# Graph convolution with residual and layer norm: zero fills read from memory, a paced order of the fills, and copies moved into the products

## The reference

```python
def _edge_conv(x, src, dst, edge_attr, W, b, denom):
    msg = jnp.concatenate([x[src], edge_attr], axis=1) @ W + b
    s = jax.ops.segment_sum(msg, dst, num_segments=x.shape[0])
    return s / denom[:, None]
...
h = _edge_conv(x, src, dst, edge_attr, W0, b0, denom)
outputs = [h]
for W, b in ((W1, b1), (W2, b2), (W3, b3)):
    cat = jnp.concatenate(outputs, axis=1)
    z = _edge_conv(cat, src, dst, edge_attr, W, b, denom)
    outputs.append(z)
return outputs[-1]
...
x = _layernorm(x + _L0_gnn_ref(...), axis=-1)
```

## Time and profile before

| | |
|---|---|
| time, median of 3 executions | 1039.77 us (1036.18 to 1040.24) |
| the profiled execution | 1047.12 us, its span 1045.2 us |
| busy share of the span | POOL 69%, DVE 67%, ACT 48%, PE 46% |
| DMA, mean over the span | 215 GB/s |
| TensorE clock granted, mean | 0.659 of full speed |

### The profile page before, as it was taken

The page is one execution under the profiler, slowest core; times in us unless marked ns, Lnnn a source line. Parts: engine busy times, 40 slices in busy tenths (PEclk is TensorE's granted clock), DMA queues, the critical chain, the costliest instruction groups (busy, mean ns, idle before and its releaser), DMA issues.

```text
span 1045.2 us, 13945 instructions
## 1 busy us (share of the span) xinstructions
PE 482.6 (46%) x3072; PEld 360.4 (34%) x3072; DVE 696.5 (67%) x2390; ACT 499.3 (48%) x1322; POOL 725.2 (69%) x660
## 2 busy tenths in 40 slices
PE   3343654877874797998663600260026563000000
PEld 2343553655653465664332500250025452000000
DVE  6995888777755696658456585757579973699000
ACT  5552674766551565666452226732675640275200
POOL 6684776777770577777576468766878774777775
PEclk9655665655655889998886655565557876555555
DMA  6799569599996356775458459985999981654111
GB/s 183 231 283 265 149 162 270 156 327 312 324 347 230 137 186 206 243 242 172 162 203 277 159 131 292 310 277 118 299 300 366 320 292 47 197 159 142 51 50 34
DMA packets 224619, 224.98 MB, mean 215 GB/s; under 512 B 19218, under 2 KB 206475, under 8 KB 224495
## 3 DMA queue, kind: packets, MB, share of 16 engines
q1 hardware_dynamic: 193551, 153.22, 47.2%
q0 software_dynamic: 26624, 44.81, 15.8%
q10 hardware_dynamic: 4320, 25.56, 6.1%
HBM read 117.11 MB, written 132.74 MB: 239 GB/s over the span
## 4 chain that ended last, share of the span: by engine, by line
DVE 20%; POOL 19%; DMA 19%; PE 17%; issue 12%; SPq 5%; ACT 5%; DVEq 2%; POOLq 0%; ACTq 0%
POOL G L670 5%; POOL out_rows L709 5%; SPq L487 4%; POOL part_rows L683 4%; DMA area<-src_low_rows 3%; DMA G<-part_rows,s0r 3%; DMA x_and_z_of_nodes<-area,sum_rows 3%; PE hp L1909 3%; DMA G<-x_in,srci 3%; PE segp L1909 2%; DVE area L1035 2%; PE hp L2049 2%; POOL G L641 2%; DVE AC L1583 2%; ACT area L809 2%
## 5 line engine op out<-in xcount | busy, mean ns | idle before, releaser
L641 POOL DMA_INDIRECT G<-x_in,srci x196 | 221.2, 1129 | 84.9 <-issue 55.6
L653 POOL DMA_INDIRECT x_and_z_of_nodes<-area,sum_rows x144 | 145.6, 1011 | 89.8 <-ACT area L809 61.7
L837 ACT ACTIVATE area<-area,AC 128x128 f32<-128x128 f32 x299 | 117.5, 479 | 43.0 <-DVE AC L1605 43.0
L778 ACT ACTIVATE UT<-segp,UT 128x1 f32 x168 | 44.0, 262 | 119.6 <-PE segp L1808 92.7
L670 POOL DMA_INDIRECT G<-part_rows,s0r x70 | 81.0, 1157 | 23.6 <-issue 18.3
L1808 PE MATMUL segp<-SX,G 128*128 128x128 f32 x336 | 83.1, 430 | 15.0 <-DMA G<-x_in,srci 11.7
L809 ACT ACTIVATE area<-hp,zero,inv 128x512 f32<-128x512 f32 x72 | 53.7, 777 | 66.6 <-DMA x_and_z_of_nodes<-area,sum_rows 32.0
L702 POOL DMA_INDIRECT EC<-x_and_z_of_nodes,idx x60 | 63.8, 1063 | 28.9 <-issue 16.5
L2043 PE MATMUL segp<-ZERO 128*128 128x390 f16 (+1 forms) x34 | 14.2, 418 | 147.4 <-DVE EC L1625 147.4
L1808 PEld LDWEIGHTS segp<-SX,G 128*128 128x128 f32 x336 | 73.3, 322 | 18.0 <-DMA G<-x_in,srci 14.2
L709 POOL DMA_INDIRECT out_rows<-UT,idx x60 | 59.1, 985 | 18.3 <-issue 17.7
(11 more groups left out here) (464 smaller groups left out, 1504.3 us busy)
## 6 DMA issues: line engine op xcount, KB each, us to landing
part_rows<-area SPq DMA_DIRECT2D x36, 768.0 KB
area<-x_and_z_of_nodes SPq DMA_DIRECT2D x30, 832.0 KB, 7.5
x_and_z_of_nodes<-ZERO SPq DMA_DIRECT2D x24, 1024.0 KB
x_and_z_of_nodes<-x_in SPq DMA_DIRECT2D x24, 1024.0 KB
area<-x_in SPq DMA_DIRECT2D x23, 832.0 KB, 7.8
out_rows<-area ACTq DMA_DIRECT2D x23, 832.0 KB, 5.1
part_rows<-ZERO SPq DMA_DIRECT2D x14, 768.0 KB
area<-src_low_rows SPq DMA_DIRECT2D x28, 224.0 KB
```

What stands on the lines that cost most here:

```text
L641: g.indirect_dma_start(G[:, slot, 0:D], None, x, bass.IndirectOffsetOnAxis(ap=srci[:, c:c + 1].bitcast(u32), axis=0), bounds_check=last_no ...
L653: g.indirect_dma_start(XZ2, bass.IndirectOffsetOnAxis(ap=sum_rows[:, c:c + 1], axis=0), HS3[:, b, j, 3 * D:4 * D], None, bounds_check=last ...
L837: last = a.activation(XLS[b][:, k], XLS[b][:, k], ACT.Identity, bias=shift[:, b, r:r + 1], scale=rs[:, b, r:r + 1])
```

## The change

It does four things. A table `ZD` (zero_rows, 128 rows of 384 zeros) is made in memory from `ZERO`, once, before the first piece, and SP waits for it; all later zeros are read from `ZD`. The order of the pieces of `clear_sums` is another: 4 at the start and 4 behind the first rows of low bits, as before; then, in place of 10 in one run ahead of the remaining 26 rows, one behind every second row (13 in all), and 4 at the end. Of `copy_x`, 12 pieces stay in the front and 13 go behind the stores of the products' steps; they count on a semaphore of their own, `copied`, for which POOL waits ahead of its last gathers. The zeros for `TB` go out behind the stores too: the part for step k in step k x 18 / 25, so that the 14 that are sent here fall into the last five steps.

```diff
-Z_AT = (4, 8, 18)
+Z_FIRST, Z_LOOKS = 8, 13
+X_FRONT = 12
...
+    ZD = nc.dram_tensor("zero_rows", [P, 3 * D], f32).ap()
...
+            e.dma_start(ZD, ZERO[:, 0:3 * D]).then_inc(s["zeros_in"], 16)
...
-                    e.dma_start(run_rows(XZ3[:, 1, :], lo, hi), ZERO[0:rows, 0:D].unsqueeze(1).to_broadcast([rows, XRUN, D])).then_inc(s["cleared"], 16)
+                    e.dma_start(run_rows(XZ3[:, 1, :], lo, hi), ZD[0:rows, 0:D].unsqueeze(1).to_broadcast([rows, XRUN, D])).then_inc(s["cleared"], 16)
...
-                    e.dma_start(run_rows(XZ3[:, 0, :], lo, hi), run_rows(x, lo, hi)).then_inc(s["cleared"], 16)
-
-            clear_sums(range(0, Z_AT[0]))
+                    e.dma_start(run_rows(XZ3[:, 0, :], lo, hi), run_rows(x, lo, hi)).then_inc(s["copied"], 16)
+
+            share = lambda n, parts, j: range(n * j // parts, n * (j + 1) // parts)
+
+            e.wait_ge(s["zeros_in"], 16)
+            clear_sums(range(0, Z_FIRST // 2))
...
-            clear_sums(range(Z_AT[0], Z_AT[1]))
+            clear_sums(range(Z_FIRST // 2, Z_FIRST))
             e.wait_ge(s["we_ready"], 1)
             for q in (0, 1):
                 load_features(q)
-            clear_sums(range(Z_AT[1], Z_AT[2]))
             for c in range(2, UNITS):
                 load_lows(c)
-            clear_sums(range(Z_AT[2], XPIECES))
+                clear_sums(Z_FIRST + p for p in share(Z_LOOKS, UNITS - 2, c - 2))
+            clear_sums(range(Z_FIRST + Z_LOOKS, XPIECES))
             for q in range(2, NQ):
                 load_features(q)
-                copy_x(range((q - 2) * XPIECES // (NQ - 2), (q - 1) * XPIECES // (NQ - 2)))
+                copy_x(share(X_FRONT, NQ - 2, q - 2))
             e.wait_ge(s["prep_done"], 1)
             n_fill = e.value_load(counts[0:1, 0:1], min_val=1, max_val=CIT)
-            for i in range(CIT):
+
+            def fill_unused(i):
                 with e.If(n_fill <= i):
                     for g in (i * 2, i * 2 + 1):
-                        e.dma_start(trows[g], ZERO[:, 0:3 * D].unsqueeze(1).to_broadcast([P, CG, 3 * D])).then_inc(s["zfill"], 16)
+                        e.dma_start(trows[g], ZD.unsqueeze(1).to_broadcast([P, CG, 3 * D])).then_inc(s["zfill"], 16)
+
...
+                copy_x(X_FRONT + p for p in share(XPIECES - X_FRONT, SLOTS, i))
+                for k in share(CIT, SLOTS, i):
+                    fill_unused(k)
                 e.sem_inc(s["tick_sp"], 1)
...
-            e.wait_ge(s["cleared"], 2 * 16 * XPIECES)
+            e.wait_ge(s["cleared"], 16 * XPIECES)
...
+            e.wait_ge(s["copied"], 16 * XPIECES)
             l_units(gather_final)
```

More of the change, by code:

```diff
@@ L355, in gnn_kernel @@
             "flags_in flags_mm order_known ld_bc ld_sort sort_dve rank_ready sorted "
-            "prep_done rows_known ut_clear zrow zfill we_ready "
+            "prep_done rows_known ut_clear zrow zeros_in zfill we_ready "
             "far row_built summed "
@@ L363, in gnn_kernel @@
             "oh_built tab_mm tab_ready os_built hot_words look_mm looked words_in a_built a_mm a_added list_ready "
-            "p_mm p_act weights_mm weights_in sc_ready cleared "
+            "p_mm p_act weights_mm weights_in sc_ready cleared copied "
             "places_known lows_turned lows_copied lows_stored chunks_ready mk_built mk_mm marked tb_ready lk_built lk_mm found2 c2_hot c2_built c2_mm c2_added "
```

## The result

The changed kernel takes 1080.95 us, the median of 4 runs (1079.54 to 1081.09); the kernel before took 1040.01 beside it (1036.18 to 1043.70). The ratio is 1.0388, with a 95% interval of 1.0345 to 1.0430: slower by 41 us, where 19 were forecast. The profiled execution took 1080.92, with a span of 1078.9.

A forecast was written before the change was run, and what follows sets the result against it. Bounds taken: row 2's wait behind ten pieces, then DVE's look-ups; in the products POOL's scatters and ACT's waits for them. Front +2, products +4 and +9, tail +4: +19 on 1047.1, 1066, or 1059 on the runs' scale; range 1033 to 1086.

The forecast's parts named there:

- The wait goes: Front: row 2 goes out at 88.8 and lands at 92.3 instead of 99.5, -7 us.
- Zeros from memory: All pieces and fills: zeros read from memory move as fast as from SBUF, priced by the copies' 323 GB/s; no difference.
- the last rival: Much slower: all pieces read the same 192 KB, a bottleneck at half the rate; +85 us, 1125; chance 0.10.
- The pacing: Look-ups: each later row pair stands behind a piece, 1.78 MB at 318 GB/s, 5.6 us a pair; +12 us.
- The front's end: End of the front: fills gone, the last gather's landing falls from 6.4 toward 3.5 us; -3, bounds 0 and -3.
- The products: Nine copies in steps 1 to 12 crowd scatters, +4 (0 to +9); stores wait behind fills in steps 13 to 17, +9.
- Behind the last store: Gap before the rounds: POOL waits for the last copy and 4 fills, first gather 15.2 us after the store; +4.
- the look-ups' share: Sign in the look-ups: the stretch should show a DMA share over 1.
- POOL's first gap after them: Sign behind the look-ups: POOL's first gap should come later by about 5 us.
- the others: Signs: DVE's chunk 2 wait 2 to 3.5 us; products +13, mostly after step 13, ACT waiting; POOL's first rounds gather awaits fills.
- The rivals of a gain: Faster: zeros from memory let the DMA engines reach 430 GB/s, the front gains 10; 1031 us; chance 0.18.
- the rival of no change: 374 GB/s throughout and scatters don't wait for copies: pacing 3, front gains 7, drain 5, tail 3; 1041 us; chance 0.16.

The follow-up runs named there:

- eight pieces ahead: The kernel before with eight instead of ten clear pieces ahead of the third row, the other two behind the rows: 1037.75 us, 0.9955.
- the four buffers: The changed kernel with four look-up row buffers instead of two: 1.0314 with zeros from the same 64 KB, 1.0229 from 1 MB of memory, 1.0191 from SBUF.
- the copies alone: The changed kernel with pieces in the old order, zeros from SBUF and fills back in the front, the thirteen copies staying with the products: 1049.30 us, 1.0067.
- The early fills: The changed kernel with pieces in the old order, zeros from SBUF, and fills sent with steps 0 to 5 instead of 13 to 17: 1062.57 us, 1.0211.
- the pacing alone: The kernel before with only the order of the clear pieces changed, thirteen paced behind every second row, zeros from SBUF: 1054.06 us, 1.0112.
- copies and fills alone: The changed kernel with the clear pieces in the old order and zeros from SBUF, copies and fills still with the products: 1062.79 us, 1.0214.

## Why the prediction was right and wrong

The direction was right, and so were the places; the size was half. By the stages, forecast and measured:

- **The wait goes**, -7: right, -6.75, and by itself it is worth 0.45% (eight pieces ahead). `ZD` and the wait for it cost nothing, as forecast: chunk 0's matrix started at 88.03 us, before at 88.19.
- **Zeros from memory**, nothing: this is the main step that failed, and the largest error, about 12 of the 22 us between forecast and measurement (1.0388 against 1.0269). The step took the copies as the nearest row. They read every line once, where a piece reads the same 64 KB sixteen times (not the 192 KB of the last rival; that is a fill). The last rival named exactly that, priced at half the rate; it is less, 270 instead of 318 GB/s in the stretch. By the four buffers it is 0.65 us a pair that goes with the repetition and 0.25 for memory as such. Why reading again is slower was not tried.
- **The pacing**, +12: the mechanism and the rate were right (5.42 us a pair at 318 GB/s when rows are early), but rows are asked for only two chunks ahead, so that the engines fall short of it: 5.97 a pair with zeros from SBUF, +17.8 from chunk 2 to 26 (71.6 less 53.8), of which 6.6 are the late asking (71.6 less the 65.0 of four buffers). The sum had no term for that wait. With zeros from memory 80.3 - 53.8 = +26.5.
- **The front's end**, -3: more, -7.4, outside its bounds (0 and -3). The last gather is late by as much as chunk 26; from it to the first scatter it takes 30.4 us instead of 37.5. With the copies alone out of the front it is 34.0, with the fills out too 30.4: so both count.
- **The products**, +4 and +9: right, together (+13.8) and each by itself (+4.3 up to step 13, +9.5 from there). ACT waited 10 us more for scatters and 15.3 for stores, as forecast.
- **Behind the last store**, +4: mis-sized, +10.6 from that store and +12.5 from the last scatter. I counted only what is issued behind that store, 4.4 MB. But the two fills, the copy and the stores of the steps before were still to be moved: SP was held 7.93 us at two fills, and the first gather came 22.0 us after the last store (592.13 less 570.16) instead of 15.2. From 570 to 590 us the DMA engines moved 350 GB/s, the forecast's rate, but 7.0 MB; some of that is SP's first loads for the layer norm, which went out from 581 us on. The early fills show the rest: the backlog that was taken away here was paid in the products.

By the mechanism, then, the forecast was right in the products and in the rate, and wrong where it took a price from copies, left out the late asking and counted a backlog too small. At the front's end it erred the other way, by 4 us, which hid part of these misses; that was luck. Of the signs, the time from chunk 2 to 26 grew to 80.3 us instead of 66, the look-ups' share stayed under 1 (0.93), and POOL's first gap after them came 19.3 us later (201.43 against 182.10) instead of 5; the others came true.

The rivals of a gain and of no change fell: from 100 to 160 us no run with thirteen paced pieces moved more than 318 GB/s, and scatters did wait. As its terms are written, the rival of no change adds up to 1044; its 1041 takes in the -3 of the front's end as well. The 323 GB/s of the copies hold the gathers too: of the 28.4 MB from 202 to 290 us SP's queue moved 24.4, so the copies moved some 277 GB/s in and the same out, and not 323; read and written together that is still over 500. The round trip with which I started after the result fell as the main cause; it holds for 6.6 us.

By the ratios on 1040 us, the pacing alone costs 12, copies and fills alone 22, and both together with zeros from SBUF 28; what is left to the 40 of the changed kernel, 12, is zeros from memory. That the two together cost 6 us less than their sum is within their intervals (some 6 us each).

## What to carry to other kernels

Before you move transfers from a full stretch to one that looks half idle, ask whether the small transfers on the critical path there are asked for early enough, and how many bytes the stretch's rate leaves: here, with four row buffers and zeros from SBUF, six pieces left the look-ups no longer than before, and thirteen made them 11 us longer (65.0 against 53.8). Bytes put into a stage whose engines wait for each other through DMA cost the same here at either place that was tried, so count all that is still queued, not only what is issued last. Don't price a transfer that reads the same lines over and over by one that reads each line once.

## What the runs showed of the hardware that was not expected

Five clear pieces in a row, with only gathers beside them, SP's queue in order of time: from the same 64 KB in the changed kernel, from SBUF, and from 1 MB of memory. The time is that for which SP's queue was held; the fifth piece is the one of 848 rows. The second row of each is the feature load behind them:

```profile
171.61 16.10 SPq L490 DMA_DIRECT2D x_and_z_of_nodes<-zero_rows  x5
188.12 23.82 SPq L477 DMA_DIRECT2D area<-ea_in  x4
```

```profile
162.51 14.98 SPq L490 DMA_DIRECT2D x_and_z_of_nodes<-ZERO  x5
177.91 22.49 SPq L477 DMA_DIRECT2D area<-ea_in  x4
```

```profile
165.06 14.78 SPq L490 DMA_DIRECT2D x_and_z_of_nodes<-zero_rows  x5
180.24 2.36 SPq L477 DMA_DIRECT2D area<-ea_in  x4
```

Back to back, reading the same 64 KB holds the queue 7 to 9% longer; between the rows, which also read the same lines for all partitions, it made a pair 11 to 17% longer (6.32 against 5.67 and 5.42).

The feature loads were held for 22 to 24 us behind the last piece, which has 53 runs of 16 rows. What the DMA engines of the changed kernel moved from 186 to 212 us, in 40 slices, falls to 21 to 23 GB/s in about half of the slices; one gather's 0.0655 MB in a slice of 0.65 us is 101 GB/s, so the slices with some 117 fit a gather beside it:

```profile
GB/s 250 263 299 333 352 347 370 294 217 89 117 22 117 23 97 42 98 42 21 23 22 22 47 22 21 22 116 22 117 21 22 117 21 117 22 117 21 61 182 159
```

With zeros read once from memory, source and target are both 848 rows in a regular pattern, and the hold is gone (2.36 us). The Trainium skill, "DMA: Bandwidth & Descriptors", in the section on why a DMA increments its semaphore by 16, says that a DMA goes to the largest number of engines up to 16 that divides the slowest dimension of both its sides. By our working that is 1 engine for 53 runs and 16 for 848 rows. The rows agree: from 197.7 to 200.3 us of the changed kernel the share was 0.07 at 22 GB/s, and a sixteenth is 0.06. The hold cost nothing here, since the last gather came 157 to 159 us after chunk 26 with the hold and without it.
